# Refilling two loads of a ring one by one, and sharing out a last step, in the last part of a graph block kernel

## The reference

```python
x = _layernorm(x + _L0_gnn_ref(x, adj, adj, Wq, Wk, Wv, Wo), axis=-1)
x = _layernorm(x + _L1_gnn_ref(x, adj, router_w, router_b, expert_w, bn_gamma, bn_beta), axis=-1)

# in _L1_gnn_ref
top1 = jnp.argmax(x.mean(axis=1) @ router_w + router_b, axis=-1)
support = jnp.einsum('bnh,bhk->bnk', x, expert_w[top1])
out = jnp.einsum('bnm,bmk->bnk', adj, support)
...
y = (out - m) * inv * bn_gamma[top1][:, None, :] + bn_beta[top1][:, None, :]
return jax.nn.relu(y)
```

## Time and profile before

| | us |
|---|---|
| median of three runs | 2787.62 |
| the profiled execution | 2794.6 |
| its span, first to last instruction | 2791.9 |
| first load of `phase_two` issued, after the span's start | 2528.7 |
| first store issued | 2568.8 |
| last load issued | 2753.1 |
| PE busy in the span | 2636.5 (94%) |
| DVE busy | 2075.6 (74%) |
| ACT busy | 1782.4 (64%) |
| POOL busy | 889.9 (32%) |

### The profile page before, as it was taken

One profiled execution on the slowest core, in us unless ns is written; L12 is line 12 of the kernel. 1 busy time (PEld: TensorE's weight loads), 2 busy tenths in 40 slices (PEclk: granted clock), 3 DMA queues, 4 the chain that ended last, 5 costly groups with the idle time before them and its releaser, 6 DMA issues. The chain is left out here.

```text
span 2791.9 us, 70332 instructions
## 1 busy us (share of the span) xinstructions
PE 2636.5 (94%) x24130; PEld 2332.5 (84%) x24130; DVE 2075.6 (74%) x3838; ACT 1782.4 (64%) x6183; POOL 889.9 (32%) x493
## 2 busy tenths in 40 slices
PE   7999999999999999999999999999999999966764
PEld 6888888888888888888888888888888888855654
DVE  6877777777777777777777777777877777753987
ACT  4666666666666666666666666666666666644977
POOL 2133232233232233232232322332222333113876
PEclk9999999999999999999999999999999999987887
DMA  6445444454454454444454444544544544457998
GB/s 246 160 177 185 155 176 169 165 184 169 158 187 159 172 188 158 169 182 158 178 181 156 178 168 166 184 165 162 188 158 173 188 158 170 160 184 316 421 411 324
DMA packets 152826, 537.82 MB, mean 193 GB/s; under 512 B 15538, under 2 KB 48306, under 8 KB 105650
## 3 DMA queue, kind: packets, MB, share of 16 engines
q1 hardware_dynamic: 152754, 536.96, 51.9%
HBM read 427.84 MB, written 109.05 MB: 192 GB/s over the span
## 5 line engine op out<-in xcount | busy, mean ns | idle before, releaser
L586 ACT ACTIVATE prob<-prob,neg_max 128x128 f32<-128x128 f32 x2048 | 791.8, 394 | 5.1 <-DVE abs_max L714 5.1
L351 POOL TENSOR_TENSOR norm<-norm,constants 128x1 f32<-128x1 f32 x128 | 70.6, 552 | 1469.0 <-DVE norm L753 1469.0
L341 POOL TENSOR_TENSOR moments<-moments,conv 128x1024 f32 x128 | 310.5, 2426 | 295.3 <-ACT conv L637 214.8
L586 ACT ACTIVATION_READ_ACCUMULATOR prob<-prob,neg_max 128x1 f32 x2048 | 394.7, 193 | 0.0
L572 ACT ACTIVATE qk<-bank 128x512 f32<-128x512 f32 x256 | 153.0, 598 | 348.0 <-PE bank L360 348.0
L686 DVE SCALAR_TENSOR_TENSOR prob<-bank,adj_in 128x512 f32<-128x512 f32 x512 | 316.8, 681 | 0.0
L360 PE MATMUL bank<-xT_hi,wq_hi 128*128 128x256 f32 x1024 | 303.0, 296 | 12.9 <-DVE wq_lo L649 11.2
L703 DVE TENSOR_TENSOR prob<-prob,inv_sum 128x2048 f32<-128x2048 f32 x128 | 302.4, 2362 | 4.4
L709 DVE TENSOR_REDUCE neg_max<-prob 128x16 f32<-128x2048 f32 x128 | 291.7, 2279 | 0.0
L714 DVE TENSOR_REDUCE abs_max<-prob 128x16 f32<-128x2048 f32 x128 | 291.6, 2278 | 0.0
L360 PE MATMUL bank<-xT_hi,wq_lo 128*128 128x256 f32 x1024 | 290.8, 284 | 0.0
(11 more groups left out here) (131 smaller groups left out, 6493.4 us busy)
## 6 DMA issues: line engine op xcount, KB each, us to landing
expert_hi<-expert_hi_scratch SPq DMA_DIRECT2D x125, 1024.0 KB, 4.9
expert_lo<-expert_lo_scratch SPq DMA_DIRECT2D x125, 1024.0 KB, 7.0
xT_in<-xT SPq DMA_DIRECT2D x64, 512.0 KB, 3.5
x_in<-x SPq DMA_DIRECT2D x128, 256.0 KB, 2.7
x_scratch<-x SPq DMA_DIRECT2D x128, 256.0 KB, 2.2
conv_scratch<-conv SPq DMA_DIRECT2D x128, 256.0 KB, 2.4
conv_in<-conv_scratch SPq DMA_DIRECT2D x32, 1024.0 KB, 9.2
x_in<-x_scratch SPq DMA_DIRECT2D x32, 1024.0 KB, 12.4
```

The source lines that it names most:

```text
L341: pool.tensor_tensor(acc, acc, conv[:, pv_mod(u, -5, 2), :, :].rearrange("p k d -> p (k d)"), ALU.add).then_inc(moments_added, 1)
L586: last = act.activation(prob[:, par2, h, :], prob[:, par2, h, :], ACT.Exp, bias=neg_max2[:, par2, h:h + 1], scale=2.0, accum_out=row_sum[: ...
```

## The change

Two semaphores take the place of one: `ld_conv_g` and `ld_x1_g`. PE waits for conv alone; DVE waits for x1 before the first join of a group. SP refills the two halves of a place at different times. Conv of group h+8 is asked for when group h has been turned (`refill_conv`, which waits for `turned`), and that stands in SP's order ahead of the store of group h-1. x1 of group h+8 is asked for as before, when the store of h has landed. SP's loop and GpSimd's last loop turn are written out. For the last group (31) GpSimd normalizes nothing; its quarters 0 and 1 go to DVE and ACT, behind the quarter that each has anyway.

```diff
+        def refill_conv(h, r, live):
+            if live(h) and live(h + RING):
+                sp.wait_ge(turned, (h + 1) * C)
+                load_conv(h + RING, r)
 
         def group(k, r, live):
             g = k * RING + r
+            if isinstance(g, int) and g == 0:
+                refill_conv(0, 0, live)
+            refill_conv(g + 1, (r + 1) % RING, live)
             if live(g):
-                sp.wait_ge(pool_finished, (g + 1) * POOL_TURNS)
-                sp.wait_ge(dve_finished, g + 1)
-                sp.wait_ge(act_finished, g + 1)
+                ends_here = isinstance(g, int) and g == NG - 1
+                sp.wait_ge(pool_finished, (g if ends_here else g + 1) * POOL_TURNS)
+                sp.wait_ge(dve_finished, g + 2 if ends_here else g + 1)
+                sp.wait_ge(act_finished, g + 2 if ends_here else g + 1)
                 sp.dma_start(by_token(out, g * G, G), flat(x1_in, r)).then_inc(st_g[r], 16)
             h, r1 = g - REFILL_LAG, (r - REFILL_LAG) % RING
             if live(h) and live(h + RING):
                 sp.wait_ge(st_g[r1], 16 * ((k if r >= REFILL_LAG else k - 1) + 1))
-                load(h + RING, r1)
-
-        for r in range(RING):
-            group(0, r, lambda g: 0 <= g < NG)
-        with sp.Fori(1, NG // RING - 1, 1) as k:
-            for r in range(RING):
-                group(k, r, lambda g: True)
-        for r in range(RING):
-            group(NG // RING - 1, r, lambda g: 0 <= g < NG)
+                load_x1(h + RING, r1)
+
+        for g in range(NG):
+            group(g // RING, g % RING, lambda g: 0 <= g < NG)
...
-                pe.wait_ge(ld_g[r], (k + 1) * 32)
+                pe.wait_ge(ld_conv_g[r], (k + 1) * 16)
...
-            for j in range(POOL_TURNS):
+            for j in range(0 if isinstance(g, int) and g == NG - 1 else POOL_TURNS):
...
-                act.activation(x1_in[:, r2, ACT_TURN, :], x1_in[:, r2, ACT_TURN, :], ACT.Identity,
-                               bias=shift[:, r2 % 2, ACT_TURN:ACT_TURN + 1],
-                               scale=rstd[:, r2 % 2, ACT_TURN:ACT_TURN + 1]).then_inc(act_finished, 1)
+                for j in (ACT_TURN, 1) if isinstance(h, int) and h == NG - 1 else (ACT_TURN,):
...
-        def join(h, r, j):
+        def join(h, r, j, k):
+            if j == 0:
+                dve.wait_ge(ld_x1_g[r], (k + 1) * 16)
             dve.wait_ge(turned_back, h * G + j + 1)
...
+            for j in (DVE_TURN, 0) if isinstance(g, int) and g == NG - 1 else (DVE_TURN,):
```

More of the change, by code:

```diff
@@ L832, in phase_two @@
     ld_bn = sem("ld_bn")
-    ld_g = [sem(f"ld_g{i}") for i in range(RING)]
+    ld_conv_g = [sem(f"ld_conv_g{i}") for i in range(RING)]
+    ld_x1_g = [sem(f"ld_x1_g{i}") for i in range(RING)]
     st_g = [sem(f"st_g{i}") for i in range(RING)]
@@ L882, in _, with load_conv, load_x1 @@
         sp.dma_start(beta_t[:, :], v["beta"].rearrange("p e c -> p (e c)")).then_inc(ld_bn, 16)
-        def load(g, r):
-            sp.dma_start(flat(conv_in, r), by_token(conv_dram, g * G, G)).then_inc(ld_g[r], 16)
-            sp.dma_start(flat(x1_in, r), by_token(x1_dram, g * G, G)).then_inc(ld_g[r], 16)
+        def load_conv(g, r):
+            sp.dma_start(flat(conv_in, r), by_token(conv_dram, g * G, G)).then_inc(ld_conv_g[r], 16)
+        def load_x1(g, r):
+            sp.dma_start(flat(x1_in, r), by_token(x1_dram, g * G, G)).then_inc(ld_x1_g[r], 16)
         for r in range(RING):
-            load(r, r)
+            load_conv(r, r)
+            load_x1(r, r)
+        def refill_conv(h, r, live):
+            if live(h) and live(h + RING):
+                sp.wait_ge(turned, (h + 1) * C)
+                load_conv(h + RING, r)
         def group(k, r, live):
             g = k * RING + r
+            if isinstance(g, int) and g == 0:
+                refill_conv(0, 0, live)
+            refill_conv(g + 1, (r + 1) % RING, live)
             if live(g):
-                sp.wait_ge(pool_finished, (g + 1) * POOL_TURNS)
-                sp.wait_ge(dve_finished, g + 1)
-                sp.wait_ge(act_finished, g + 1)
+                ends_here = isinstance(g, int) and g == NG - 1
+                sp.wait_ge(pool_finished, (g if ends_here else g + 1) * POOL_TURNS)
+                sp.wait_ge(dve_finished, g + 2 if ends_here else g + 1)
+                sp.wait_ge(act_finished, g + 2 if ends_here else g + 1)
                 sp.dma_start(by_token(out, g * G, G), flat(x1_in, r)).then_inc(st_g[r], 16)
@@ L967, in group @@
             pool.sem_inc(rstd_seen)
-            for j in range(POOL_TURNS):
+            for j in range(0 if isinstance(g, int) and g == NG - 1 else POOL_TURNS):
                 pool.tensor_scalar(x1_in[:, r, j, :], x1_in[:, r, j, :], mean_var[:, r % 2, j, 0:1],
                                    rstd[:, r % 2, j:j + 1], ALU.subtract, ALU.mult).then_inc(pool_finished, 1)
-        run_groups(pool, group, 0)
+        for r in range(RING):
+            group(0, r, lambda g: 0 <= g < NG)
+        with pool.Fori(1, NG // RING - 1, 1) as k:
+            for r in range(RING):
+                group(k, r, lambda g: True)
+        for r in range(RING):
+            group(NG // RING - 1, r, lambda g: 0 <= g < NG)
     @block.scalar
@@ L1000, in group @@
                 act.wait_ge(shift_made, h + 1)
-                act.activation(x1_in[:, r2, ACT_TURN, :], x1_in[:, r2, ACT_TURN, :], ACT.Identity,
-                               bias=shift[:, r2 % 2, ACT_TURN:ACT_TURN + 1],
-                               scale=rstd[:, r2 % 2, ACT_TURN:ACT_TURN + 1]).then_inc(act_finished, 1)
+                for j in (ACT_TURN, 1) if isinstance(h, int) and h == NG - 1 else (ACT_TURN,):
+                    act.activation(x1_in[:, r2, j, :], x1_in[:, r2, j, :], ACT.Identity,
+                                   bias=shift[:, r2 % 2, j:j + 1],
+                                   scale=rstd[:, r2 % 2, j:j + 1]).then_inc(act_finished, 1)
         run_groups(act, group, 2)
@@ L1054, in finish @@
                                      in1=rstd[:, r % 2, :], op0=ALU.mult, op1=ALU.mult).then_inc(shift_made, 1)
-            dve.tensor_scalar(x1_in[:, r, DVE_TURN, :], x1_in[:, r, DVE_TURN, :], mean_var[:, r % 2, DVE_TURN, 0:1],
-                              rstd[:, r % 2, DVE_TURN:DVE_TURN + 1], ALU.subtract,
-                              ALU.mult).then_inc(dve_finished, 1)
+            for j in (DVE_TURN, 0) if isinstance(g, int) and g == NG - 1 else (DVE_TURN,):
+                dve.tensor_scalar(x1_in[:, r, j, :], x1_in[:, r, j, :], mean_var[:, r % 2, j, 0:1],
+                                  rstd[:, r % 2, j:j + 1], ALU.subtract, ALU.mult).then_inc(dve_finished, 1)
         def take_stats(h, r, j):
@@ L1065, in group @@
             if live(h):
-                join(h, r1, 0)
-                join(h, r1, 1)
+                join(h, r1, 0, k)
+                join(h, r1, 1, k)
                 take_stats(h, r1, 0)
-                join(h, r1, 2)
+                join(h, r1, 2, k)
                 take_stats(h, r1, 1)
@@ L1073, in group @@
             if live(h):
-                join(h, r1, 3)
+                join(h, r1, 3, k)
                 take_stats(h, r1, 2)
```

## The result

The changed kernel takes 2782.1 us (median of 13 runs), the kernel before 2789.0 us (13 runs). The ratio is 0.9977, with a 95% interval from 0.9969 to 0.9984. That is 6.4 us less by the ratio (4.5 to 8.6; the two medians alone are 6.9 apart), with 7.6 us forecast. The profiled execution has a span of 2784.5 us, where 2784.3 was forecast. That close a match is partly luck: several terms were wrong and cancelled, as the rest shows.

The account below looks back on a forecast made before the run. Mostly not bound by DMA: VectorE's pace of 6.2 us a group, with TensorE waiting for loads in the last groups. Terms -5.9 + 1.0 - 2.7 = -7.6 us gave a median of 2780.0 us, range 2777.5 to 2786.5.

Parts of the forecast that it names:

- (a): Last groups: x becomes what paces them, as a wait in VectorE; 2785.9 us if the whole gain there goes; chance 0.22.
- (c): ScalarE's loop starts: code-fetch pauses grow with two more transfers in flight; up to +7.4 us, 2795.0 us; chance 0.09.
- Part 1: Last groups: conv and x on their own semaphores, conv refilled once turned, end TensorE's waits for loads; -5.9 us.
- x's lead: Groups 29 to 31: x lands ahead of its join by 5.6, 7.0 and 8.0 us.
- 2765.46 less the hole: Group 31's x: lands at 2761.8, as filling the DMA gap near 2572 saves 3.6 us.
- Part 2: VectorE's first join of each group: the added wait for x costs +1.0 us, bounds 0.6 to 3.1.
- Part 3: Group 31: moving GpSimd's two quarters to ScalarE and VectorE issues the last store sooner; -2.7 us.
- (b): SP's single list: conv refills stand behind waits for earlier stores, so conv isn't asked for when turned; 2785.9 us; chance 0.07.

Follow-up runs that it names:

- e3: The changed kernel with the last group's two quarters back on GpSimd; ratio to the kernel before 0.9978.
- e1: The kernel before with the two semaphores alone, refills and last steps as they were; ratio 0.9988.
- e9: The kernel before with the two semaphores and SP's and GpSimd's loops written out, conv and x still refilled together at the old place; ratio 0.9996.
- e2_last: The kernel before with only the last group's two quarters moved from GpSimd to ScalarE and VectorE; ratio 0.9993.
- b2_before: The kernel before run once more, unchanged, for a second profile; ratio 0.9999.
- e4: The kernel before with one more, already passed wait on VectorE before each group's first join; ratio 0.9998.
- e6: The changed kernel with ScalarE's loop written out and experts' numbers read one group ahead everywhere; ratio to the kernel before 0.9949, 2774.6 us.
- e8_both: The changed kernel with ScalarE's loop written out and three quarters of each refill of x left out; ratio to the kernel before 0.9916.

## Why the prediction was right or wrong

**The total.** -7.6 us forecast, -6.4 us measured; 2780.0 forecast and 2782.1 measured, inside the range. As a case it was the forecast one: TensorE lost its waits, and none of the rivals (a) to (c) took the gain. The span came out within 0.2 us because errors cancelled. Between the two profiled executions group 26 came 3.4 us earlier, which was not forecast, and the new wait cost nothing in place of 1.0; against that the five steps to group 31 took 1.9 us more than forecast, and the end behind the last store 2.7 us more.

**Part 1, -5.9 us forecast.** The split and the early refill together are e3: 0.9978, -6.1 us. The size holds (-8.9 to -3.3), but its make-up doesn't. The split alone, which should have brought nearly all of it, brings 3.3 us in e1 and 1.1 in e9. The term was read from one execution. There, five group steps took 36.86 us; in three other executions of what is in effect the same kernel up to there they took 36.3 (e2_last), 33.6 and 32.0, against 31.0 at the pace. So the waits cost 5.9, 5.3, 2.6 and 1.0 us, 3.7 in the mean. The step that failed is the taking of one profile as the size of the waits at the end. That it was a slow execution, 5.6 us above the median of the 13 runs, isn't what made them long: e2's profiled execution took 2786.0 us and had nearly the same. The two traces with the long waits are those in which join 24 came earlier (198.4 and 197.1, against 199.5 and 199.4), so that TensorE came earlier to loads that were not there yet.

The early refill was priced at nothing but room for x, and brought the other half or more. Part of that is conv itself, which with the split alone can still come late (e9). The rest shows in ScalarE's pauses, which the prediction held fixed and rival (c) had growing. The changed kernel, starts of groups 8, 16 and 24:

```profile
2601.13 3.05 ACT L1007 ACTIVATE bnT<-bank,shift_t,scale_t 128x128 f32<-128x128 f32 x8 [0.30 <-PE bank L944]
...
2658.30 5.70 ACT L1007 ACTIVATE bnT<-bank,shift_t,scale_t 128x128 f32<-128x128 f32 x16 [6.19 <-issue]
...
2715.09 5.71 ACT L1007 ACTIVATE bnT<-bank,shift_t,scale_t 128x128 f32<-128x128 f32 x16 [6.14 <-issue]
```

And b2_before:

```profile
2600.01 5.75 ACT L993 ACTIVATE bnT<-bank,shift_t,scale_t 128x128 f32<-128x128 f32 x16 [3.85 <-issue]
...
2658.78 5.75 ACT L993 ACTIVATE bnT<-bank,shift_t,scale_t 128x128 f32<-128x128 f32 x16 [7.81 <-issue]
...
2716.58 5.85 ACT L993 ACTIVATE bnT<-bank,shift_t,scale_t 128x128 f32<-128x128 f32 x16 [7.27 <-issue]
```

The idle time at group 8 falls from 3.9 to 0.3 us, though ScalarE starts the group only 1.8 us sooner (73.2 and not 75.0, counted as in the table), since what it does before ends later. At group 16 it falls from 7.8 to 6.2 us. This holds in every trace with ScalarE's loop: at group 8 the idle time is 0.3 to 1.5 us in the four with the early refill and 3.4 to 3.9 in the six without it, at group 16 6.2 to 6.5 against 7.5 to 8.3. At group 24 the two don't differ (6.1 to 8.5 against 6.1 to 8.0). In the pause ScalarE reads four experts' numbers into registers. These reads, from the trace by line (ns, shortest, median, longest) around the start of group 16, in the kernel before:

```profile
L979 ACTq TENSOR_LOAD <-expert_of x5: 286/612/1009, 2657.0 to 2661.8; - x5
```

And in the changed kernel:

```profile
L993 ACTq TENSOR_LOAD <-expert_of x7: 273/283/662, 2655.6 to 2661.1; - x7
```

At the old place of the refills the reads take 0.61 us in the median, in the changed kernel 0.28. The four reads ahead of group 16 take 2.3 to 2.8 us together in the six traces without the early refill and 1.1 to 1.4 in the four with it, while the idle time ahead of the first of them is 3.3 to 4.1 us in both. So the reads are the part of the pause that shrinks. That it is the early refill that shortens it is shown as far as e9 and e3 differ in little else. Why the reads get shorter is argued and not shown: probably by which transfers are in flight at those instants.

**x's lead, forecast 5.6 to 8.0 us.** It was 0.1 to 2 us in groups 29 to 31 of the changed kernel's two traces. The count of transfers ahead of the last x (89) was right and the hole was filled, but three transfers took 8.0 us in both traces and 7.7 to 7.8 in those of the kernel before. Over 14 groups that is 3 to 5 us, about what the hole gave, and the new hole near 2750 took up to 1.5 us more. The step that failed is "2765.46 less the hole": it took the rate as fixed and the queue as full to the end. Why the rate falls isn't settled. e3_nolast, which issues the same transfers in the same order up to the last store, had 7.70, and its last x landed at 234.5, where 234.0 was forecast. In the six traces with the old order and ScalarE's loop the last x lands anywhere from 234.6 to 238.5. So much of it differs from execution to execution and isn't shown to come from the order of the refills. The kernels without ScalarE's pauses had 7.5, so the pauses may have a part in it.

**Part 2, +1.0 us forecast.** Nothing, by e4. The step that failed is the reading of 0.02 us from the earlier trace rows as the price of an instruction in sight, and then adding margin to it. The rows don't bear it: the join starts 0.08 and 0.10 us after the start of a variance that lasts 0.17 us, so the two overlap and there is no idle time to price. That VectorE passes such a wait while the instruction before it still runs would fit this, but no run shows it.

**Part 3, -2.7 us forecast.** The time from the last variance to the last store was right to 0.1 us (3.1 us, in all six traces with the new last steps). The condition that the prediction itself wrote down, "The store must find the queue empty", failed: the stores of groups 25 to 31 stand in one row behind the last x, and they drain at one in 2.5 us. Issued 2.7 us sooner, the last store takes 6.5 and 5.9 us and not 3.8 to 4.2. It was worked out that 94 transfers would have landed by 2774.3; with the last x landing 5 us later than forecast, they hadn't. In e3's trace, where x was on time, they had landed by 247.3.

**Rivals.** (a) was there in part, as a wait of 1.14 us on VectorE, and it is what holds e6. (b) didn't decide: conv was always early, though the stores of finished groups did wait on SP's one list. Group 25's store was issued at 2757.64, 16 us after GpSimd had done its part. The rule of the Trainium skill named there (Perfetto Trace Analysis, DMA Optimizations: loads on one issuing engine, stores on another) wasn't tried, and no run here shows it. (c) went the other way, since the pauses got shorter. Its rule of the Trainium skill (Runtime: NRT & Kernel Launch, Instruction fetch mechanics: a taken branch to code that isn't held forces a fetch) agrees with e6: with ScalarE's loop branches gone the pauses are gone. But the four reads that stood in them are gone from there too, so the share of the fetch isn't shown apart.

## What to carry to other kernels

If two inputs of a step share a semaphore, the engine that reads only one of them waits for both. Splitting them is cheap, but how much it gives depends on how late each input is: 3.3 us in one kernel here and 1.1 in another. When compute and transfers end within a few microseconds of each other, a gain on one side is worth only the distance to the other: the same 18 MB were worth 1.4 us in one kernel and 9.2 us in its sibling, and the same written-out loop 4.5 us and 8.4 us (these last two aren't clear of the noise from each other). Filling one hole in the queue can open another further on, so look at who issues next once a kind of transfer has run out. And where a forecast rests on waits of a few microseconds, read them in more than one execution; here the same waits cost 5.9, 5.3, 2.6 and 1.0 us in four.

## What the runs showed of the hardware that was not expected

- A read of one number from on-chip memory into a register of ScalarE takes from 0.27 us up to 1.3 to 1.5 us (kernel before, two traces) and 1.5 to 1.6 us (changed kernel, two traces) in the last part, where the DMA share is mostly 1.0; its mean over the 128 reads is 0.45 to 0.53 us in all complete kernels, and 0.41 us in e8_both, which moves the least data.
- The time in which the same 3 MB of two loads and a store move isn't fixed with the DMA share at 1.0: it is 7.48 to 8.04 us in the traces of kernels that move the same data, 7.70 and 7.82 in two executions of the kernel before, and 7.70 to 8.04 in three of the changed order. What it depends on is open.
- A wait that is already passed costs VectorE nothing that can be seen, at a pace of 6.2 us a group: with one more wait a group the steps stay at 6.21 us (e4_wait).
